# Cross-attention with image tokens on one core: bias in the output projection, statistics of 64 columns, context loads by GpSimd, one spread of the values a batch, residual added by VectorE

## The reference, cut to what matters

```python
q = split_heads(x @ w_q)                       # x: 64 batches x 256 rows x 320
k, v = split_heads(text @ w_k), split_heads(text @ w_v)        # text: 69 rows of 512 a batch
out_text = softmax(q k^T / 4) v                # 20 heads of 16
k_ip, v_ip = the same from the last 8 rows of the context, with w_k_ip, w_v_ip
out_ip = softmax(q k_ip^T / 4 + mask_ip) v_ip  # mask from the boxes
out = (out_text + out_ip) @ w_out + b_out + x
```

## Time and profile before

| | |
|---|---|
| median of 3 runs | 1270.41 us (1267.28 to 1271.23) |
| span of the profiled execution, from its first to its last instruction | 1263.2 us |
| busy: PE, DVE, ACT, POOL | 1158.1, 1044.3, 897.6, 904.7 us |
| mean granted TensorE clock | 0.979 of full |

### The profile page before, as it was taken

The page is one execution under the profiler, slowest core; times in us unless marked ns, Lnnn a source line. Parts: engine busy times, 40 slices in busy tenths (PEclk is TensorE's granted clock), DMA queues, the critical chain, the costliest instruction groups (busy, mean ns, idle before and its releaser), DMA issues.

```text
span 1263.2 us, 34240 instructions
## 1 busy us (share of the span) xinstructions
PE 1158.1 (92%) x12734; PEld 1114.9 (88%) x12734; DVE 1044.3 (83%) x2054; ACT 897.6 (71%) x1923; POOL 904.7 (72%) x1004
## 2 busy tenths in 40 slices
PE   6998887559999999999999999999999999999996
PEld 5898787459999999999999999999999999999985
DVE  5687975669888889888898888888888888898972
ACT  2343343448888888877888888888888888887773
POOL 0111101038889889988988988898898899898896
PEclk9999999779999999999999999999999999999998
DMA  6388887645555545544455554454555555555431
GB/s 173 66 181 168 156 182 149 102 91 111 116 116 120 120 114 121 120 115 114 114 120 120 121 117 115 115 116 115 117 117 115 118 120 117 123 117 114 102 82 61
DMA packets 361460, 151.31 MB, mean 120 GB/s; under 512 B 298640, under 2 KB 350864, under 8 KB 360016
## 3 DMA queue, kind: packets, MB, share of 16 engines
q1 hardware_dynamic: 361296, 149.13, 52.9%
HBM read 88.17 MB, written 39.90 MB: 101 GB/s over the span
## 4 chain that ended last, share of the span: by engine, by line
PE 53%; POOL 11%; DMA 11%; SPq 9%; DVE 6%; issue 5%; ACT 2%; POOLq 0%; ACTq 0%; DVEq 0%
PE ps_a L832 9%; DMA q_hi_extra<-q_hi_lo 8%; PE ps_o L903 8%; PE ps_s L873 7%; PE ps_m L854 6%; PE ps_s L879 6%; PE ps_b L832 6%; POOL prob_lo L1402 6%; PE ps_k L199 2%; PE ps_v L199 2%; SPq L617 2%; SPq L668 2%; POOL y L1396 2%; DMA x_keep<-in_x_dram 2%; PE ps_a L918 2%
## 5 line engine op out<-in xcount | busy, mean ns | idle before, releaser
L1402 POOL TENSOR_TENSOR prob_lo<-prob,prob_hi 128x512 f16<-128x512 f32 (+1 forms) x448 | 506.1, 1148 | 106.0 <-ACT prob_hi L1071 106.0
L873 PE MATMUL ps_s<-q_hi_lo,keys 128*128 128x256 f32 x960 | 248.9, 299 | 44.3 <-DMA q_hi_extra<-q_hi_lo 42.9
L1070 ACT ACTIVATE prob<-ps_s 128x512 f32<-128x512 f32 (+1 forms) x448 | 254.2, 567 | 35.4 <-PE ps_s L879 31.0
L1071 ACT ACTIVATE prob_hi<-ps_s 128x512 f16<-128x512 f32 (+1 forms) x448 | 252.8, 564 | 0.0
L879 PE MATMUL ps_s<-q_hi_extra,keys 128*128 128x256 f32 x960 | 234.1, 281 | 0.3 <-ACT q_hi_extra L1058 0.3
L1298 DVE TENSOR_REDUCE stats<-ps_m 128x8 f32<-128x552 f32 x320 | 231.2, 722 | 0.0
L873 PEld LDWEIGHTS ps_s<-q_hi_lo,keys 128*128 128x128 f32 x960 | 172.6, 190 | 54.1 <-issue 37.4
L903 PE MATMUL ps_o<-values,prob_hi 128*128 128x68 f16 (+7 forms) x3584 | 200.9, 193 | 1.5 <-DVE heads L1312 1.5
L903 PE MATMUL ps_o<-values,prob_lo 128*128 128x68 f16 (+3 forms) x1792 | 190.8, 193 | 0.0
L903 PEld LDWEIGHTS ps_o<-values,prob_hi 128*128 128x128 f16 x3584 | 174.9, 98 | 13.0 <-issue 1.6
L879 PEld LDWEIGHTS ps_s<-q_hi_extra,keys 128*128 128x128 f32 x960 | 173.5, 190 | 0.5 <-ACT q_hi_extra L1058 0.5
(11 more groups left out here) (180 smaller groups left out, 2999.1 us busy)
## 6 DMA issues: line engine op xcount, KB each, us to landing
x_in<-in_x_dram SPq DMA_DIRECT2D x64, 320.0 KB, 3.8
q_hi_extra<-q_hi_lo SPq DMA_DIRECT2D x64, 320.0 KB, 3.4
x_keep<-in_x_dram SPq DMA_DIRECT2D x64, 320.0 KB, 3.2
out_dram<-y SPq DMA_DIRECT2D x128, 160.0 KB, 1.8
k_scratch<-k_stage SPq DMA_DIRECT2D x16, 770.0 KB, 5.8
keys<-k_scratch SPq DMA_DIRECT2D x256, 48.1 KB, 2.1
ctx_in<-in_ctx_dram SPq DMA_DIRECT2D x64, 128.0 KB, 2.8
keys<-k_scratch SPq DMA_DIRECT2D x256, 24.1 KB, 1.9
```

Source lines behind the costliest of these rows:

```text
L873: mm(ps, keys[:, n, 0, quad, c:c + P], q_hl[n][:, quad, :], start=i == 0, stop=False)
L1070: nc.scalar.activation(prob[:, s, 0:w], ps_s[(b[1] + s) % 2][:, 0:w], ACT.Exp)
L1071: nc.scalar.activation(prob_hi[par(b)][:, s, 0:w], ps_s[(b[1] + s) % 2][:, 0:w], ACT.Exp).then_inc(s_hi, 1)
L1402: nc.gpsimd.tensor_tensor(prob_lo[par(b)][:, s, 0:w], prob[:, s, 0:w], prob_hi[par(b)][:, s, 0:w], ALU.subtract).then_inc(s_lo, 1)
```

## The change

Five parts, and some moves with them.

1. **Bias.** The third term of the output projection, `wo[1]` rows 0 and 32, holds the bias in two parts, and `aT2[1]`, now a tile of its own, has ones in these rows. `aT2[0]` holds all 128 rows of the third transposed piece. POOL's `add_bias` goes.
2. **Residual.** ACT's `y_out` and POOL's `finish` go. DVE's new `result(t)` adds `ps_a` or `ps_b` to `x_keep` and writes `y`. `x_transpose` and the stores wait for it.
3. **Statistics** of 64 columns in rows 0 to 63 of the transposed tile; the third piece of x is 64 columns and loaded once.
4. **Context loads** by POOL's queue; the two pairs' transposes stand ahead of the two value projections.
5. **One value spread** of 2080 columns behind the second `maxima`, where three parts stood before.
6. **Moves.** SP has another order in a step; stores are issued a step later. Steps -2 and -1 become `first`, which holds the last value projection too, and `copy_q` of batch 0 stands ahead of the loads of batch 1. The 13 late tails go to the ends of steps 2 to 8, one or two a step, with stores in steps 3 to 9.

```diff
                         if n is None or n >= 2:
-                            pe.wait_ge(s_ye, at(b, NT, -3 * NT))
+                            pe.wait_ge(s_yr, at(b, NT, -3 * NT))
...
+                        def result(t):
+                            dve.wait_ge(s_op, at(d, NT, t + 1))
+                            if t == 0:
+                                dve.wait_ge(s_xk[par(d)], nth(d, 16))
+                                if n >= 4:
+                                    dve.wait_ge(s_y[par(d)], nth(d, 32, -32))
+                            nc.vector.tensor_tensor(y[par(d)][:, t, :], (ps_a, ps_b)[t][:, 0:D], x_keep[par(d)][:, t, :],
+                                                    ALU.add).then_inc(s_yr, 1)
...
-                        def finish(t):
-                            pool.wait_ge(s_ye, at(d, NT, t + 1))
-                            if t == 0:
-                                pool.wait_ge(s_xb, at(d, 1, 1))
-                            nc.gpsimd.tensor_tensor(y[par(d)][:, t, :], y[par(d)][:, t, :], x_keep[par(d)][:, t, :],
-                                                    ALU.add).then_inc(s_yr, 1)
...
-                        def add_bias():
-                            pool.wait_ge(s_xk[par(c)], nth(c, 16))
...
-                        terms += [(both, w[n][:, 2, cols]) for n in range(2)]
+                        terms += [(third_hi, w[0][:, 2, cols]), (third_lo, w[1][:, 2, cols])]
...
-                        if A:
-                            copy_q(off(b, 1))
...
+                        if n + 1 < NB:
                             copy_q(off(b, 1))
+                        if 0 <= n - 3 < NB:
+                            store(off(b, -3), 0)
+                            store(off(b, -3), 1)
+                        if 0 <= n - 1 < NB:
+                            load_residual(off(b, -1))
+                        if 3 <= n + 2 < NB:
+                            sp.wait_ge(s_sc, at(b, PAIRS, 0))
+                            load_keys(off(b, 2))
+                        if 2 <= n + 2 < NB:
+                            sp.wait_ge(s_vx, at(b, 1, 1))
+                            load_values(off(b, 2))
+                        if n + 4 < NB:
                             sp.wait_ge(s_xt, at(b, 1, 3))
                             load_x(off(b, 4))
...
                     for i in range(NI):
+                        for u in range(2):
+                            if 2 * i + u + 4 < 2 * NI:
+                                pool.wait_ge(s_t, 2 * i + u + 1)
+                                pool.wait_ge(s_sum, 2 * i + u + 1)
+                                load_pair(pool, 2 * i + u + 4)
...
+                        if 0 <= n - 2 < len(TILES_IN):
+                            tail_lo(1, n - 2)
```

More of the change, by code:

```diff
@@ L491, in xattn_kernel @@
                 s_tst = sem("tail_values_stored")
+                s_late = [sem(f"late_tail_values_stored{q}") for q in range(2)]
                 s_kz = sem("tail_keys_zeroed")
@@ L1030, in step @@
                         e, a, c, d = off(b, 2), off(b, 1), off(b, -1), off(b, -2)
-                        def x_hi():
-                            act.wait_ge(s_xt, at(e, 1, 1))
-                            nc.scalar.copy(xT[0][:], ps_a[:].rearrange("p (k s) -> p k s", k=2)).then_inc(s_xhi, 1)
-                            nc.scalar.copy(xT2[0:64, :], ps_b[0:64, 0:S]).then_inc(s_xhi, 1)
-                        def q_hi(m):
-                            act.wait_ge(s_q, at(e, 3, m + 1))
-                            ps = (ps_a, ps_b, ps_a)[m]
-                            for o in range(KW[m] // QD):
-                                nc.scalar.copy(q_hl[third(e)][0:QD, 2 * m + o, :], ps[o * QD:(o + 1) * QD, 0:S]).then_inc(s_qhi, 1)
+                        if n < 0:
+                            if n == -1:
+                                first(e, a)
+                            return
                         def a_hi():
@@ L1261, in _ @@
-                    nc.vector.memset(stats[:, :, R_ONE:R_ONE + 1], SHIFT).then_inc(s_z, 1)
-                    dve.wait_ge(s_z, 2)
+                        if i + 1 < NI:
+                            for u in range(2):
+                                context_lo(2 * (i + 1) + u)
+                            v_lo(2 * i)
+                            for u in range(2):
+                                sum_context(2 * (i + 1) + u)
+                            v_lo(2 * i + 1)
+                        prepare_main(i)
@@ new lines, in x_lo @@
+                    def x_lo(e):
+                        dve.wait_ge(s_xhi, at(e, 2, 1))
+                        nc.vector.tensor_tensor(xT[1][:], ps_a[:].rearrange("p (k s) -> p k s", k=2),
+                                                xT[0][:].bitcast(fp32), ALU.subtract).then_inc(s_xlo, 1)
+                        dve.wait_ge(s_xhi, at(e, 2, 2))
+                        nc.vector.tensor_tensor(xT2[64:P, :], ps_b[0:DL, 0:S], xT2[0:64, :].bitcast(fp32),
+                                                ALU.subtract).then_inc(s_xlo, 1)
@@ new lines, in image_maxima, with first @@
+                    def image_maxima(a):
+                        dve.wait_ge(s_dve, at(a, QUADS, QUADS))
+                        nc.vector.tensor_reduce(stats[:, :, R_MI:R_MI + H], ip_masked[:], AX.X, ALU.max).then_inc(s_ip, 1)
+                    def first(e, a):
+                        x_lo(a)
+                        for u in range(2):
+                            v_lo(2 * (NI - 1) + u)
+                        for m in range(3):
+                            q_lo(a, m)
+                        maxima(a, 0)
+                        x_lo(e)
+                        maxima(a, 1)
+                        maxima(a, 2)
+                        q_lo(e, 0)
+                        maxima(a, 3)
+                        maxima(a, 4)
+                        image_maxima(a)
+                        q_lo(e, 1)
+                        q_lo(e, 2)
@@ L1276, in q_lo @@
-                        def q_lo(m):
-                            ps = (ps_a, ps_b, ps_a)[m]
-                            for o in range(KW[m] // QD):
-                                dve.wait_ge(s_qhi, at(e, QUADS, 2 * m + o + 1))
-                                nc.vector.tensor_tensor(q_hl[third(e)][QD:P, 2 * m + o, :], ps[o * QD:(o + 1) * QD, 0:S],
-                                                        q_hl[third(e)][0:QD, 2 * m + o, :].bitcast(fp32), ALU.subtract).then_inc(s_qlo, 1)
-                        def maxima(h4):
-                            find_maxima(h4)
-                            if n in (-1, 0) and 4 * (n + 1) + h4 < (4, 7)[n + 1]:
-                                tail_lo(1, 4 * (n + 1) + h4)
```

373 lines of the change are left out of this document (206 added, 167 removed).

## The result

The changed kernel takes 1302.72 us in the median (1301.92 to 1303.0, 4 runs), the kernel before 1268.85 (1264.58 to 1271.23, 4 runs): a ratio of 1.027, 95% interval 1.0243 to 1.030. The profiled execution has a span of 1300.9 us against 1263.2, 37.7 more. The prediction, 1302, was right in sum. Its terms were less so, and two of my readings about what surrounds the stall were wrong, as the experiments show.

The account below looks back on a forecast made before the run. PE's own 14.71 us a step plus 0.66 of a POOL, SP, DMA, PE chain was taken as the bound; 1263.2 + 68 + 7 - 14 - 24 - 5 = 1295, with 7.2 to the median 1302 us, 8-in-10 range 1248 to 1328.

Parts of the forecast that it names:

- The steady stall: At x_transpose in 60 steps: PE waits 1.8 us for DVE's result(1), a step takes 16.5 us, +68 us.
- The bounds of the stall: Range for PE's wait at x_transpose: 1.3 us a step (+38) to 2.4 us (+104).
- DVE's idle time does not lie between `a_lo` and the fourth `maxima`: In the steady step of the kernel before: argument against the banks being freed in time, though DVE is only 83% busy.
- The period before: Steady step before the change: 15.37 us, PE's own 14.71 plus 0.66 of a chain POOL, SP, DMA, PE.
- That is PE without a stall: Step 25 of the kernel before: its 14.71 us taken as PE's own time, unchanged by the change.
- Late tails: Ends of steps 2 to 8: 13 instructions each on ACT and DVE delay a_hi and a_lo, +7 us (0 to 12).
- the clock falls: Rival, steady steps: new stalls bring half clock for 3 us in each step, +90 us, 1390 us; chance 0.03.
- Context iterations: Before the steps: loads on POOL's queue and transposes first cut PE's waits, -14 us (-22 to 0).
- The rival of the start: Context iterations: loads issued by POOL land no earlier, term 0 or +5 instead of -14, about 1318 us; chance 0.13.
- Entry: Into the steps: PE's 14.3 us wait for copy_q of batch 0 goes and late tails leave, -24 us (-15 to -28).
- End: Last steps: no POOL addition for y, no x_transpose in steps 62 to 64, -5 us (-2 to -8).
- The 7.2 us between span and median: Whole kernel: median stands 7.2 us above the profiled span, added to the sum of 1295 to give 1302.

Follow-up runs that it names:

- run 1: Changed kernel with VectorE's result(1) right behind result(0), ahead of norm(0): 1227.09 us, ratio 0.967 to the kernel before.
- run 3: Changed kernel with only the residual part undone (ScalarE copies out of PSUM, GpSimd adds): 1208.9 us, ratio 0.9535 to the kernel before.
- Run 2: Changed kernel with the value spread moved behind x_lo on VectorE: 1314.72 us, ratio 1.037 to the kernel before.
- Run 11: Kernel before with y stores and residual loads a step later, add_bias at the end of GpSimd's step: 1244.12 us, ratio 0.9825 to the kernel before.
- run 4: Changed kernel with the context loads back on SP's queue, ahead of each iteration's stores: 1314.3 us, ratio 1.036 to the kernel before.
- run 7: Changed kernel with transposes and value projections in turn again, loads left on GpSimd: 1306.47 us, ratio 1.032 to the kernel before.
- run 6: Changed kernel with late tails inside their step, ScalarE's ahead of x_hi, VectorE's behind x_lo: 1297.58 us, ratio 1.025 to the kernel before.
- run 9: Changed kernel with the residual part undone, first q copy and batch 1 keys early, late tails one a step: 1197.75 us, ratio 0.946 to the kernel before.

## Why the prediction was right, and where it was not

- **The steady stall: mechanism right, size 16 us too large.** `x_transpose` has an idle of 1.44 us ended by `result` on `ps_b`, run 1 and run 3 take it away by two different ways, and both gain what the stall cost. The term was 1.8 and measured 1.53, so +52 and not +68. (Against run 3's 14.62 the stall is 1.62, and 0.09 a step are a gain in TensorE's own step, for which I took nothing.) In times from `a_hi`: from the first `result` to `norm` 0.40 start to start instead of 0.52; the third `maxima` 0.1 earlier; `x_transpose` at 7.32 instead of 7.53; and TensorE stood ready at 5.88 instead of 5.73. The spread took the 1.56 that was predicted, `result` 0.47 and 0.48 for 0.49. The bounds of the stall were added up loosely: by their own terms they are 1.2 and 2.7, where 1.3 and 2.4 stand.
- **"DVE's idle time does not lie between `a_lo` and the fourth `maxima`": right for the changed kernel, but read too far afterwards.** From it I took the spread for a full term of the sum, one that would come back if it were moved. Run 2 showed that a wait for TensorE of 0.86 appears in its place. Taking an instruction out of a chain without idle time gains its duration only until something else is waited for.
- **The period before: step half right.** I read 15.37 - 14.71 as the POOL, SP, DMA chain alone. Run 11 gives that chain 0.35 of the 0.66. "That is PE without a stall" was not quite so either: run 3 comes to 14.62. The sum did not suffer, since it was made with the measured 15.37 and 14.71.
- **Late tails: mis-sized, +7 against +13.8.** The 0.4 us by which `a_hi` comes late and the 0.7 by which `a_lo` follows were there (`a_lo` 1.37 behind `a_hi` in the step at 338.59, else 0.72). Two things were missing. In steps 3 to 9 the spread takes 2.04 to 2.17 us instead of 1.56, since it meets GpSimd's operations at another point, and `x_transpose` comes 1.1 us later behind `a_hi` (8.45 instead of 7.33), 0.65 by `a_lo` and 0.47 by the spread: 7 times 0.47 is 3.3. And the two stretches at half clock are 3.0. The rival "the clock falls" had a small part after all, in 2 of 60 steps.
- **Context iterations: right.** The last key projection stands 15.9 us earlier (-14 predicted). The rival of the start, that another issuing engine gains nothing, fell: the loads are worth 11.5 us (run 4), the order of transposes some 4 (run 7). The Trainium skill (DMA: Bandwidth & Descriptors, "Issuing engines are not separate DMA queues") says that only the time of issue is saved. The trace agrees that it is time of issue, but here it is not small, since the issuer is saturated: 2.7 us of each iteration, on an SP that from 45 to 212 us of the kernel before waits for other engines in 13 of 167 us.
- **Entry: wrong step.** "The 14.3 us of rows 14 go" failed. `copy_q` of batch 0 stands behind the last stores only, as I wrote, but I gave these stores and the copy itself no time. TensorE was ready for the scores at 224.4, near the predicted 223 and 21.8 us earlier than before (246.3). SP issued the stores only from 224.73 on, for 6 us, and the copy, issued at 230.76, let TensorE go 4.2 us later. 10.5 of the 14.3 stayed. From the last key projection on, the entry gained 9.7 us, not 24.
- **End: -2.6 instead of -5.**
- **The 7.2 us between span and median: 5.3 too large.** The profiled execution of the changed kernel took 1302.79 us with a span of 1300.9, 1.9 more, and the recorded executions of the kernel before stand 2.1 to 2.2 above their spans. By that the profiled one, with a span of 1263.2, took about 1265.3, and the other 5 of the 7.2 us were the scatter between executions.

Four errors of 16, 7, 12 and 2.4 us left 6 in the sum: the span was 1295 by the sum and 1300.9 by the trace. The two larger ones, too much stall and too much gain at the entry, cancelled each other for the most part, and the fifth, of 5.3, took the rest away. That 1302 was met to the microsecond is luck, and the ranges given for the terms were the honest part. Of the rivals, that the banks are freed in time is what run 3 made true and run 1 nearly so: 1209 and 1227 us.

## What to carry over

When an engine takes over the freeing of a buffer for which TensorE waits, put the freeing instruction ahead of everything in its queue for which nobody waits: moving one statement was worth 76 us, twice the damage of the change. When a wait ends on a DMA issued by a busy queue, moving that one DMA ahead moves the wait to the next item: add up the issue times of the queue first. Look for room to move work into in a steady step, never in one of the disturbed ones at the start. And read the granted clock of each step before you put a difference down to the instructions that were moved: most of what the first steps gave back in runs 6 and 9 was clock.

## What was not expected of the hardware

The same VectorE instruction with two SBUF inputs takes very different times by what GpSimd does beside it. All 64 spreads of the changed kernel, min, median and max in ns:

```profile
L1427 DVE TENSOR_TENSOR values<-raw_v,own_rows x64: 1245/1564/2170, 241.6 to 1270.7; 128x2080 f16<-128x2080 f16 x64
```

The rows of GpSimd at the start of the spread at 608.79 and of the longest one, at 322.59, say how much:

```profile
608.09 1.17 POOL L1497 TENSOR_TENSOR prob_lo<-prob,prob_hi 128x512 f16<-128x512 f32 x1 [2.63 <-ACT prob_hi L1127]
...
322.49 1.17 POOL L1497 TENSOR_TENSOR prob_lo<-prob,prob_hi 128x512 f16<-128x512 f32 x1
322.59 2.17 DVE L1427 TENSOR_TENSOR values<-raw_v,own_rows 128x2080 f16<-128x2080 f16 x1
```

GpSimd's operation ends 0.47 us into the first of these spreads and 1.07 into the second. The spreads take 1.56 and 2.17, that is 1.10 behind the end of GpSimd's operation both times. So a spread costs what is left of the operation under way, and then its own 1.1 us (the shortest, 1.24, starts ahead of GpSimd's operation). GpSimd's next operation, begun at 609.21, takes 2.18 us instead of 1.17 and ends 1.04 behind the spread, so it seems to wait in its turn. The small tails (32 partitions, 320 columns) are stretched more in proportion than the large spread: from 0.54 to 1.35 us for the second of each pair in run 6, and to as much as 1.31 in run 9. `result`, with one input in PSUM, took 473 to 483 ns in all 96 of its rows from 420 to 1200 us. The issue time of a DMA does not go by its bytes: SP needs 1.5 us in the mean to issue a store of values of 80 KB, and 0.5 to 0.8 for the copy of q of 320 KB. Nor is it fixed by the shape: the four stores issued from 224.73 on, all alike, take 0.6 to 3.4 us each.
